# Selective scans: first turn in halves on free banks with softplus on VectorE, Silu from PSUM, six B row buffers copied four states ahead

## The reference, cut to what matters

```python
xz = einsum('bld,ed->ble', hidden, in_proj_w)
x, z = xz[..., :256], xz[..., 256:]
x_conv = silu(causal_conv4(x, conv_w) + conv_b)
x_dbl = einsum('bld,ed->ble', x_conv, x_proj_w)
dt_in, Bv, Cv = split(x_dbl, [64, 16, 16])
delta = softplus(einsum('blr,dr->bld', dt_in, dt_proj_w) + dt_proj_b)
A = -exp(A_log)                                    # 256 x 16
h = h * exp(delta_t * A) + (delta_t * x_conv_t) * B_t   # for each token t
y_t = einsum('bdn,bn->bd', h, C_t)
y = (y + x_conv * D) * silu(z)
out = einsum('bld,md->blm', y, out_proj_w)
```

## Time and profile before

| | us |
|---|---|
| median of 3 executions | 3884.96 (3879.69 to 3885.21) |
| the profiled execution | 3883.17 |
| its span in the trace | 3881.3 |
| busy: TensorE, VectorE, ScalarE, POOL | 3227.5, 2305.5, 1684.3, 1129.1 |
| VectorE scans (line 2079), 384 of them | 445.4 busy, 155.2 idle before them |
| POOL products with B (line 1978), 192 | 448.8 busy, 57.7 idle before them |
| copies of row B by ScalarE (line 1920), 192 | 578 ns each (median) |

### The profile page before, as it was taken

How to read it: one execution, slowest core, us unless ns; L and a number is a source line. 1 busy time by engine, 2 the same in 40 slices (tenths; PEclk the granted TensorE clock), 3 DMA queues, 4 the chain that set the end, 5 groups by cost and what they waited for, 6 DMA issues and landing times. The chain is left out here.

```text
span 3881.3 us, 60926 instructions
## 1 busy us (share of the span) xinstructions
PE 3227.5 (83%) x21852; PEld 1681.0 (43%) x21852; DVE 2305.5 (59%) x5868; ACT 1684.3 (43%) x3473; POOL 1129.1 (29%) x611
## 2 busy tenths in 40 slices
PE   7889899997777777989688896788779887788778
PEld 3444444445666666434233342233234333354336
DVE  5666445446666666465288403898861257954991
ACT  3444433313222222233476425676642455543562
POOL 1000000001111111000389204999940105740871
PEclk8999999895555555999799997999999898999999
DMA  4323231220000000022200000000000100140114
GB/s 135 98 78 94 67 95 41 60 83 14 0 0 0 0 0 0 15 75 70 85 1 0 1 0 0 1 1 1 0 1 0 79 1 33 76 159 36 65 76 174
DMA packets 76652, 166.57 MB, mean 43 GB/s; under 512 B 9553, under 2 KB 46545, under 8 KB 67921
## 3 DMA queue, kind: packets, MB, share of 16 engines
q1 hardware_dynamic: 76496, 164.64, 12.6%
HBM read 120.57 MB, written 44.04 MB: 42 GB/s over the span
## 5 line engine op out<-in xcount | busy, mean ns | idle before, releaser
L1203 PE MATMUL psum<-h_ring,h_parts 128*128 128x4 bf16 (+2 forms) x12288 | 439.1, 170 | 163.7 <-ACT h_ring L1261 157.4
L2079 DVE TENSOR_TENSOR_SCAN s_hh<-psum,s_dbu 128x512 f32<-128x512 f32 x384 | 445.4, 1204 | 155.2 <-POOL s_dbu L1978 101.2
L1203 PEld LDWEIGHTS psum<-h_ring,h_parts 128*128 128x128 bf16 x12288 | 382.8, 105 | 222.4 <-ACT h_ring L1261 192.0
L1978 POOL TENSOR_TENSOR s_dbu<-s_du,s_bb 128x1024 f32<-128x1024 f32 x192 | 448.8, 2355 | 57.7 <-ACT s_bb L1920 54.2
L1261 ACT ACTIVATE h_ring<-h_pre 128x16 f32<-128x16 f32 x1024 | 175.2, 212 | 486.7 <-DVE h_pre L1331 481.0
L1805 PE MATMUL psum<-s_term,w_c 128*128 128x512 f32 x768 | 382.0, 613 | 0.0
L1935 ACT ACTIVATE psum<-s_delta,s_decay 128x512 f32<-128x512 f32 x384 | 263.3, 690 | 149.6 <-DVE s_hh L2079 142.8
L1331 DVE TENSOR_REDUCE h_pre<-psum 128x16 f32<-128x48 f32 x1024 | 170.8, 203 | 135.5 <-PE psum L1203 125.5
L872 DVE TENSOR_TENSOR f_hid<-f_gate,psum 128x512 f32<-128x512 f32 x184 | 126.1, 686 | 202.3 <-PE psum L798 194.7
L859 ACT ACTIVATE f_gate<-psum 128x512 f32<-128x512 f32 x184 | 109.7, 597 | 285.4 <-PE psum L794 285.3
L863 POOL MEMSET r_weights<- 128x512 f32 x4 | 2.1, 524 | 758.6 <-POOLq L3081 456.9
(11 more groups left out here) (449 smaller groups left out, 6424.9 us busy)
## 6 DMA issues: line engine op xcount, KB each, us to landing
x_spill<-x_flip SPq DMA_DIRECT2D x28, 1024.0 KB, 3.8
f_share<-f_wide SPq DMA_DIRECT2D x208, 128.0 KB, 3.0
a_ks<-a_spread SPq DMA_DIRECT2D x96, 128.0 KB, 2.8
a_qs<-a_spread SPq DMA_DIRECT2D x96, 128.0 KB, 2.8
x_spare<-x_spill SPq DMA_DIRECT2D x4, 2048.0 KB, 7.6
x_raw<-x_spill SPq DMA_DIRECT2D x4, 2048.0 KB, 8.0
x_norm<-x_spill SPq DMA_DIRECT2D x4, 2048.0 KB, 8.1
w_l3f<-in_l3f SPq DMA_DIRECT2D x1, 7240.0 KB, 19.9
```

Of the source, the lines that this page charges most:

```text
L1203: mm = nc.tensor.matmul(columns_of(s // BLOCK, grp)[:, s % BLOCK, 0:3 - part, cols], parts[:, part, GROUP * grp + p, :], upper[:, (s - 1) ...
L1978: nc.gpsimd.tensor_tensor(dbu[:, s % 4], du[:, t % 2], both(bb[:, s % 4, :]), ALU.mult).then_inc(dbu_ready, 1)
L2079: nc.vector.tensor_tensor_scan(hh[:, s % 4, half, :], DECAYS[i % 3], dbu[:, s % 4, half, :], 0.0, ALU.mult, ALU.add).then_inc(scan_done, 1)
```

## The change

- **Banks.** For rows below EARLY = 3 - BR (two rows in the first scan layer, one in the second) the convolution's halves go to two banks (CONV), and the gates to two others (GATES); turn 0's delta arguments as well (RATES).
- **Silu from PSUM.** For these rows ScalarE applies Silu with the bias straight from the bank, half by half, to u and z. Later rows are made as before.
- **First turn.** It is written out in each queue instead of being run through the slots. Exp, Ln and the inverse are done half by half; 1 + e is a VectorE operation, and (grow - 1) - mag another, in place of two ScalarE operations and one POOL operation; the rest of softplus, and `du`, are VectorE's. The sign of the lost part is turned, and the last operation subtracts. POOL starts with its first product with B.
- **Order.** TensorE doesn't wait for `skip_ready` and `minus_ready` until it uses what they stand for. Row 1 (first scan layer only): its first convolution half stands in turn 0's last wait, its second half and gates after the first pick of B; its Silus, between two table loads, stand after the copies of the B rows 0 to 3 and the first decay of state 1.
- **B rows.** `bb` has six buffers, and `pick_b` and `keep_b` are called four states ahead. The ring of POOL's products keeps its four, and its calls stay two ahead.

```diff
     DECAYS = (bank[1], bank[4], bank[5])
     KEPT = 4 - BR
+    EARLY = 3 - BR
+    B_RING, B_AHEAD = 6, 4
...
-        bb = sb("s_bb", [P, 4, CHUNK])
+        bb = sb("s_bb", [P, B_RING, CHUNK])
...
+        CONV = ((PRE, bank[1]), (bank[6], bank[7]))
+        GATES = ((bank[4], bank[5]), (bank[3], PRE))
+        RATES = (bank[1], bank[4])
+        def u_there(eng, b):
+            if b < EARLY:
+                eng.wait_ge(conv_kept, 2 * b + 2)
+            else:
+                eng.wait_ge(u_ready, b + 1 - EARLY)
...
-                norm.tensor(pe)
-                pe.wait_ge(g.loaded[pack], 16)
-                pe.wait_ge(norm.normed, 1)
-                pe.wait_ge(taps_ready, 1)
-                pe.wait_ge(minus_ready, 1)
-                pe.wait_ge(skip_ready, 3)
+                def first_conv(b, half):
+                    for k in reversed(range(TAPS)):
+                        late = TAPS - 1 - k
+                        mm = nc.tensor.matmul(CONV[b][half][:, late:], w["taps"][:, (2 * k + half) * P:(2 * k + half + 1) * P],
+                                              fixed(g.normed, b)[:, 0:CHUNK - late], start=(late == 0), stop=(k == 0))
+                    mm.then_inc(conv_ready, 1)
+                def first_gates(b):
+                    for half in range(2):
+                        if b and half:
+                            pe.wait_ge(lo_kept, 1)
+                        nc.tensor.matmul(GATES[b][half], w["in"][:, (2 + half) * P:(3 + half) * P], fixed(g.normed, b),
+                                         start=True, stop=True).then_inc(z_there, 1)
+                def first_turn():
+                    rank, rows = ranks[0], 96 if ranks[0] > 32 else 64
+                    pe.wait_ge(conv_kept, 2)
+                    for half in range(2):
+                        mm = nc.tensor.matmul(PRE[0:rows, :], w["xall0"][:, half * rows:(half + 1) * rows], u[:, 0, half, :],
+                                              start=(half == 0), stop=(half == 1))
+                    mm.then_inc(parts_ready, 1)
+                    for half in range(2):
+                        pe.wait_ge(dt_kept, 1)
+                        if half:
+                            pe.wait_ge(z_kept, 1)
+                        nc.tensor.matmul(RATES[half], w["dtw0"][:, half * P:(half + 1) * P], dt[0:rank, :],
+                                         start=True, stop=True).then_inc(delta_ready, 1)
+                    pe.wait_ge(minus_ready, 1)
+                    pe.wait_ge(hi_kept, 1)
+                    nc.tensor.matmul(bc_rows(0), neg[0:32, 0:32], bc[0:32, 0, :],
+                                     start=False, stop=True, skip_group_check=True).then_inc(mid_ready, 1)
+                    for b in range(1, EARLY):
+                        first_conv(b, 0)
+                    pe.wait_ge(mid_kept, 1)
+                    nc.tensor.matmul(bc_rows(0), neg[0:64, 32:64], bc[0:64, 0, :],
+                                     start=False, stop=True, skip_group_check=True).then_inc(lo_ready, 1)
...
                 def pick_c(s):
                     t, n = divmod(s, N)
+                    if s == 0:
+                        pe.wait_ge(z_kept, 2 * EARLY)
...
+                        else:
+                            pe.wait_ge(skip_ready, 3)
+                            pe.wait_ge(conv_kept, 2 * EARLY)
...
-                for s in range(SLOTS):
-                    row_part(0, s)
-                for s in range(SLOTS):
-                    slot(-1, s)
+                norm.tensor(pe)
+                pe.wait_ge(g.loaded[pack], 16)
+                pe.wait_ge(norm.normed, 1)
+                pe.wait_ge(taps_ready, 1)
+                first_conv(0, 0)
+                first_conv(0, 1)
                 pe.wait_ge(norm.normed, CHUNKS)
+                first_gates(0)
+                first_turn()
                 pe.wait_ge(tables_cast, 2)
-                for s in range(3):
+                pick_b(0)
+                for b in range(1, EARLY):
+                    first_conv(b, 1)
+                    first_gates(b)
+                for s in range(1, B_AHEAD):
                     pick_b(s)
                 for s in range(STEPS + 3):
                     t, n = divmod(s, N)
-                    if s + 3 < STEPS:
-                        pick_b(s + 3)
+                    if s + B_AHEAD < STEPS:
+                        pick_b(s + B_AHEAD)
...
                 def keep_b(s):
                     act.wait_ge(b_spread, s + 1)
-                    if s >= 4:
-                        act.wait_ge(dbu_ready, s - 3)
-                    nc.scalar.copy(bb[:, s % 4, :], PICK_B).then_inc(b_kept, 1)
+                    if s >= B_RING:
+                        act.wait_ge(dbu_ready, s - B_RING + 1)
+                    nc.scalar.copy(bb[:, s % B_RING, :], PICK_B).then_inc(b_kept, 1)
...
+                    if i < 3:
+                        act.wait_ge(z_kept, 2)
+                    if i == 0:
+                        act.wait_ge(f_delta, 1)
+                    elif n == 0:
                         act.wait_ge(delta_done, t + 1)
...
+                def first_silu(b, half):
+                    act.wait_ge(conv_ready, 2 * b + half + 1)
+                    nc.scalar.activation(u[:, b, half, :], CONV[b][half], ACT.Silu, bias=w["conv_b"][:, half:half + 1]).then_inc(conv_kept, 1)
+                def first_gate(b, half):
+                    act.wait_ge(z_there, 2 * b + half + 1)
+                    nc.scalar.activation(z[:, b, half, :], GATES[b][half], ACT.Silu).then_inc(z_kept, 1)
+                def first_rate(half):
+                    act.wait_ge(delta_ready, half + 1)
+                    bias = w["dtb0"][:, half:half + 1]
+                    nc.scalar.activation(delta[:, 0, half, :], RATES[half], ACT.Relu, bias=bias).then_inc(pos_kept, 1)
+                    nc.scalar.activation(mag[:, half, :], RATES[half], ACT.Abs, bias=bias).then_inc(mag_kept, 1)
+                def first_exp(half):
+                    act.wait_ge(mag_kept, half + 1)
+                    nc.scalar.activation(mag[:, half, :], mag[:, half, :], ACT.Exp, scale=-1.0).then_inc((f_exp, exp_done)[half], 1)
+                def first_log(half):
+                    act.wait_ge((f_grown, grown)[half], 1)
+                    act.wait_ge((f_lost, lost)[half], 1)
+                    nc.scalar.activation(grow[:, half, :], grow[:, half, :], ACT.Ln).then_inc((f_log, log_done)[half], 1)
+                def first_inverse(half):
+                    act.wait_ge((f_log, log_done)[half], 1)
+                    nc.scalar.activation(inv[:, half, :], grow[:, half, :], ACT.Exp, scale=-1.0).then_inc((f_inv, inv_done)[half], 1)
+                nc.scalar.preload_act_table_set("silu_and_others")
+                first_silu(0, 0)
+                first_silu(0, 1)
+                act.wait_ge(parts_ready, 1)
+                nc.scalar.copy(dt[0:ranks[0], :], PRE[0:ranks[0], :]).then_inc(dt_kept, 1)
+                first_gate(0, 0)
+                nc.scalar.copy(bc[0:32, 0, :], bc_rows(0)).then_inc(hi_kept, 1)
+                first_gate(0, 1)
+                first_rate(0)
+                first_rate(1)
+                nc.scalar.preload_act_table_set("natural_log_exp_and_others")
+                first_exp(0)
+                first_exp(1)
+                act.wait_ge(mid_ready, 1)
+                nc.scalar.copy(bc[32:64, 0, :], bc_rows(0)).then_inc(mid_kept, 1)
+                first_log(0)
+                first_inverse(0)
+                first_log(1)
+                first_inverse(1)
+                act.wait_ge(lo_ready, 1)
+                nc.scalar.copy(bc[64:96, 0, :], bc_rows(0)).then_inc(lo_kept, 1)
                 act.wait_ge(norm.normed, CHUNKS)
                 keep_b(0)
                 decays(0, 0)
                 decays(0, 1)
-                keep_b(1)
-                keep_b(2)
+                for s in range(1, B_AHEAD):
+                    keep_b(s)
+                if EARLY > 1:
+                    decays(1, 0)
+                    nc.scalar.preload_act_table_set("silu_and_others")
+                    for b in range(1, EARLY):
+                        for half in range(2):
+                            first_silu(b, half)
+                        for half in range(2):
+                            first_gate(b, half)
+                    nc.scalar.preload_act_table_set("natural_log_exp_and_others")
                 for s in range(STEPS):
                     t, n = divmod(s, N)
-                    if s + 1 < STEPS:
+                    if s + 1 < STEPS and (s or EARLY == 1):
                         decays(s + 1, 0)
                     if s >= 1 and not by_vector(s - 1):
                         keep_c(s - 1)
                     slot(t, 2 * n)
                     if s + 1 < STEPS:
                         decays(s + 1, 1)
-                    if s + 3 < STEPS:
-                        keep_b(s + 3)
+                    if s + B_AHEAD < STEPS:
```

(36 more changed lines are left out.)

24 lines of the change are left out of this document (12 added, 12 removed).

## The result

| | before | after | ratio after / before |
|---|---|---|---|
| time, median of 4 runs (us) | 3882.62 (3879.69 to 3885.21) | 3833.32 (3828.60 to 3836.76) | 0.9872, interval 0.9855 to 0.9890 |
| profiled execution: time, span (us) | 3883.17, 3881.3 | 3836.76, 3834.9 | |

What follows compares the result with a forecast made beforehand. Two selective-scan layers were taken as bound by a latency-bound start and a saturated part pinned by state 8's C copy. 18.4 + 22.5 + 1.5 = 42.4 us off gave 3840.8 or 3842.6, stated as 3842; own range 3833 to 3853, wider 3829 to 3862.

Steps and rivals of the forecast that it cites:

- The sum: Both scan layers: 18.4 us in the first, 22.5 in the second and 1.5 from B rows, 42.4 us in all.
- Convolution: Start of both scan layers: without the pause, two halves at full clock take 7.1 us; bound 12.6 at low clock.
- the first rival: Low clock in both starts: gains become 6.5 and 12.3 us, with 1.5, giving 3865 us; chance 0.12.
- From dt to the exponential: Scan layer start: eight ScalarE operations of about 0.6 us to 1888.1, table load 1.28, first Exp done at 1890.05.
- Softplus on VectorE: Scan layer start: VectorE ends du at 1898.1; first scan at 1900.5 instead of 1929.33, 28.8 us earlier.
- a start's gain as kept whole: Scan layer starts: everything after the first scans depends on them, not on fixed times, so what is cut is kept.
- What the first layer still owes: First scan layer: second row's work moves behind the first scan; ten of 28.8 us given back, state 2 18.4 us earlier.
- The second layer: Second scan layer, nothing owed: first scan at 2372.9 against 2395.69; 22.5 us gained after a C pick 0.3 late.
- Six B rows: Ten softplus-preparing turns: B waits end, but state 8's C copy holds POOL; 0.15 us each, 1.5 in all.
- a turn longer or shorter by over 0.5 us: Sign of being wrong: a turn was to stay as long as now, within 0.5 us.
- The rival of 21 us: B ring worth more: with an earlier C copy, POOL's waits would be path, 21 us more, 3822; chance 0.07.
- Double loads: Rival: each of four table loads on the new path costs another 1.28 us, gain 5.1 less, 3848; chance 0.03.

Runs made afterwards that it cites:

- spare_buffers: Kernel before with six B row buffers allotted and only four used, so only places in SBUF change; 3884.24 us, ratio 1.0004.
- pool_last: Changed kernel with the first turn's last sum, product, subtraction and du back on POOL, 1024 wide; 3829.09 us, ratio 0.9864.
- no_ring: Changed kernel with four B row buffers and copies three states ahead, as before the change; 3833.89 us, ratio 0.9873.
- conv_early: Changed kernel with row 1's second convolution half moved right behind its first half in TensorE's queue, first scan layer only; 3829.21 us, ratio 0.9862.
- term_six: Changed kernel with POOL's products with C at states 3, 6 and 13 instead of 3, 8 and 13; 3813.29 us, ratio 0.9820.
- far_ahead_eight: Changed kernel with conv_early's edit, B copies five ahead, POOL's B products three ahead in a ring of six, C products at 3, 8, 13; 3825.32 us.
- ring_only: Kernel before with only the six B row buffers and the copies four states ahead; 3873.61 us, ratio 0.9976.

## Why the prediction was right, step by step

- *The sum.* 18.4 + 22.5 + 1.5 were forecast; the traces have 21.7 + 22.9 by state 2 and 2.0 later. The time came out 8.7 us under the forecast of 3842, at the edge of its own range of 3833 to 3853. That the second start fits to 0.4 us is partly luck: the forecast took both starts of before as they stood in one execution, and against those of spare_buffers the gains are 18.6 and 25.1. Their sum is 0.9 smaller.
- *Convolution.* 7.1 us at full clock with the pause gone: 7.01 in both layers. The low clock in the convolution of the starts, the first rival, did not come. With the pause put back alone the first scan comes 3.2 us later in one layer and 6.2 in the other. So the reason was sound as a forecast (no pause, full clock), but a pause does not always bring the low clock. The rival's own sum had a slip: 12.6 - 7.1 is 5.5 for the convolution, not 5.9. And 3862, called half the way to it, is 20 of its 23 us.
- *From dt to the exponential.* The load was to end and Exp to start 16.5 us behind the norm; it started at 16.24.
- *Softplus on VectorE.* du was to end 25.2 behind the norm and ended at 24.30. The one-source add, which no row of before had, takes 0.43, between the bounds 0.35 and 0.69. First scan at 26.92, forecast 27.6. pool_last measures the last four operations of this step alone: 5.3 us of the first scan. But only 2.65 of them reach the end, and only in the second layer. The prediction took a start's gain as kept whole; here it is not quite, and without the ring (no_ring against before) the second layer keeps 21.3 of the 23.3 us that it has by state 2.
- *What the first layer still owes* was right as a mechanism and is the term that was mis-sized: 10.4 us given back were forecast, and it is 29.5 - 21.7 = 7.8. State 2 was forecast 44.2 us behind the norm and came at 40.9, 3.3 earlier. I priced the late convolution half at the low clock for its whole length, 6.8 (rows 2 had 6.32 at a granted clock of 0.58); it took 5.28 at a mean granted clock of 0.67. It also began 0.7 us earlier, 21.6 behind the norm instead of 22.3, which makes 2.2 of the 3.3 us. The gates and the copies after it (copies 1.06 apart, not 1.25) are another 0.7; the last 0.4 were not followed. conv_early shows the block is the limit of that start: moving this half alone gave 3.76 us.
- *The second layer.* 22.5 forecast, 22.9 measured; on the split see the first point.
- *Six B rows.* 1.5 us forecast; 3.1 measured in the layers, by taking the ring out. The argument held: POOL's waits moved from the B copies to the C copy, ten operations of POOL follow it without a gap, and term_six and far_ahead_eight show that the place of state 8's product is what pins the turn. But the prediction named a turn longer or shorter by over 0.5 us as a sign of being wrong, and three of the ten distances are shorter by more: 62.65 to 61.19 in the first layer (61.44 in no_ring, so the ring has 0.25 of it), 61.52 to 59.93 and 60.55 to 59.91 in the second. The 61.52 us turn held long waits for B copies (up to 2.35 us in no_ring), which I missed. The rival of 21 us was wrong here but not far from what the ring is worth (15 to 19) once the pin is gone.
- *Double loads.* The prediction cited the Trainium skill, page "ScalarE: Activation LUTs", section "What ACT_TABLE_LOAD costs", for a drain of about 1380 ns on top of a load. The traces decide against it here: the loads at 1889.24 and 1906.47 take 1.28 each, and the next operation starts 0.01 and 0.02 behind them.

## What to carry to other kernels

Time a latency-bound start by what the steady state first waits for, not by its first operation: 5.3 us of earlier first scan were worth nothing in one layer here and half of themselves in the other. When one wait of a shared turn is removed and the turn stays as long, look for the event behind which an engine's operations run without a gap; move that event, and the removed wait may then be worth several times as much (the ring: 3 us with the pin, 15 without it). When a kernel changes by a few tenths of a percent, read the stages whose code changed, and look whether the others moved too. A pause ahead of a burst of matmuls has to be priced with both clocks, since the same pause can cost only itself or twice that.

## What was not expected of the hardware

- Layers whose code is the same in all these kernels took 3015.9 to 3018.1 us together in three profiled executions (ring_only, pool_last, conv_early) and 3023.4 to 3026.8 in the other ten. For ring_only it also shows in the medians of eleven or more runs: it is 9.3 us faster with 3.45 in the layers that it changes. The new places of the buffers alone do not do it (spare_buffers). Where it lies can be seen. The sixth layer took 111.9 us in the kernel after and 108.6 in conv_early, and nearly all of that is one burst of the same matmuls. These are the rows of that burst for the two kernels, first after, then conv_early, with TensorE's granted clock in such a stretch (0.55 and 1.00) beneath each:

```profile
1607.78 2.05 PE L794 MATMUL psum<-normed,w_l1f 128*128 128x512 f32 x2
1606.90:1613.70 6.80, 6.80 (x13) 0.55 0.00 0
...
1602.04 1.11 PE L794 MATMUL psum<-normed,w_l1f 128*128 128x512 f32 x2
1601.40:1604.90 3.50, 3.50 (x15) 1.00 0.00 0
```

  So at least this part of the difference is the TensorE clock, which stood near its low level in one of the two kernels and was full in the other, at a place where their code is the same. What decides it is open, and so is whether the kernel or the execution does; small ratios were therefore read here by the layers.
- A pause of 2.9 us left the clock at full speed in one start (7.08 for two halves) and lowered it in the other (10.14). The kernel before shows the same. Behind a pause of 3.04 us its first convolution half took 6.32 us in the first layer; in spare_buffers, the same code, it took 3.66:

```profile
1876.98 3.66 PE L1718 MATMUL psum<-normed,w_l2a 128*128 128x512 f32 x8 [3.04 <-DVE s_through L2046]
```

  In the second layer it is the other way round, 5.36 us before and 6.64 in spare_buffers. That is why the starts of these two differ by 3.1 and 2.2 us. The Trainium skill, page "TensorE: Matmul & The Clock Gate", section "What's actually happening", says that the monitor behind the gate runs free of the kernel, so that the point where the clock changes varies. These rows agree with that, and no run here tests it.
